# Attention block: the newest chunk's first piece waits for less, upsampling additions at other steps, rectifier inside VectorE's last additions

## The chip, the cores and the metric

The kernel runs on one core of one Trainium2 chip. Its five engines work from queues of their own and wait for one another by semaphores: TensorE (PE in the rows; PEld is its weight load), VectorE (DVE), ScalarE (ACT), GpSimd (POOL) and SyncE (SP), which here only starts transfers. The metric is the time of one execution on the device in microseconds. Tiles live in SBUF; matmuls write into eight PSUM banks.

## The reference

Input `x` is 4 images of 256 channels of 128 x 128, in float32. Each goes through this:

```python
shortcut = x
out = bilinear_resize(x, H // 2, W // 2)
out = relu(bn(conv1x1(out, conv1_w), bn1_s, bn1_b))
out = att(out, q_w, q_b, k_w, k_b, v_w, v_b, att_gamma)   # softmax(q^T k) over 64*64 positions
out = relu(bn(out, bn2_s, bn2_b))
out = bn(conv1x1(out, conv2_w), bn3_s, bn3_b)
out = bilinear_resize(out, H, W)
return relu(out + shortcut)
```

Attention runs over 4096 positions with 32 channels for queries and keys and 256 for values. All of it is computed to float32 accuracy; the kernel splits weights of the softmax and values into high and low halves of 16 bits.

## The kernel before

**Batches and blocks.** Every image is a batch `b` with two parts. `enter(b)` computes the first convolution, queries, keys and values of the batch. Then eight blocks `n` (also called chunks; `c` is 0, 1 or 7 and says which program text is used, and `g = b * 8 + n`) take 512 query positions each. A block has 32 steps `t`, one for each 128 keys. What each engine does in a step is written out by hand in its `blk`.

**TensorE in a step.** For four row tiles `it` it multiplies `ph` (high halves of the weights) by `vh` and `vl`, and `pl` (low halves) by `vh`, into `acc[it]` (lines 1062 to 1064). After row tile 2 it makes the energies of step t + 3 in `et`, two banks in turn (L940), which wait until `pl` of the step two before is made. Most steps also have one or two pair units (L928), which find the maxima for the next block in banks `emx` and `wrk`. Steps 30 and 31 are merged. The transposes of the block before come at steps 1 and 5 (L952), its second convolution at 20 and 22 (L960).

**ScalarE.** For each step it takes two exponentials of `et` (L443, L444), and for each pair of units the positive part `above` (L452). In between stand the batch norm and rectifier `relu_h` (L456), `bn3`, which writes the convolution's result into `win` and counts `y_rdy` up twice a chunk (L475), the copies of `osb` (L574), the final rectifier of upsampled pieces (L481) and the stores (L486).

**VectorE.** In its iteration t it makes `pl` of step t + 2 (`low_parts`, L710), at every second unit `pair_max` (L689, a custom operation), at steps 2 and 6 the `residual` (L720), at 31 the reciprocals of row sums (`row_sum`, L809) and its copy of `osb` (L830), and last in an iteration, what `T_ADD` puts there.

**Pieces.** Each block also upsamples four pieces j of chunks finished earlier, of 8 output rows each. GpSimd computes `up_chain` (L335 to L352): row differences `rd` and `rt`, then `y2`, `cd` and `ct`. There is one `y2` and one `ct`, so `y2` of the next piece waits for the first two additions of the piece before, and `ct` for the last two. Then VectorE adds `y2` to the two halves of the shortcut rows in `xres` (parts 0 and 1, L737) and `ct` to the same halves (parts 2 and 3, L740). Part 0 waits for the whole `up_chain`. `T_ADD[j][part]` gives the step. ScalarE rectifies at `T_RELU[j]` and stores one step later; piece 3 is rectified at step 1 of the next block. Pieces 0 to 2 are of the chunk three back, piece 3 of the chunk two back. There are no pieces 0 to 2 before block 3 and no piece 3 before block 2 of batch 0.

**Downsampling.** Between the pieces, in the first three batches, GpSimd downsamples four pieces of the next batch (`down_piece`, L315 to L325), so its order is up 0, down 0, up 1, down 1, up 2, down 2, up 3, down 3. SP loads their inputs into `xin` and the shortcuts into four slots of `xres`; a slot's load waits for the store of what was in it.

**The end.** In the last block two more pieces are added by `T_ADD_LAST`. Nine late pieces follow after TensorE's last work, shared by GpSimd and VectorE; VectorE makes all their additions, ScalarE rectifies and stores.

Of the kernel before, what the change touches and what calls it, by code (L numbers as in the profile page):

```python
# [18 lines left out]
NB = N // IB  # L19
# [14 lines left out]
SHIFT = 256.0  # L34
V_TOP = 2.0 ** 14
BN = 1.0 / (1.0 + 1e-5) ** 0.5

DN, DV, UP = 6, 5, 5
V_OF = (3, 2, 3, 2, 2, 2, 2, 2)
# [2 lines left out]
def attention_block_kernel(nc, x, w1, s1, b1, wq, bq, wk, bk, wv, bv, gamma, s2, b2, w2, s3, b3,  # L42
                           ident_d, down_w, up_w, out):
    with ExitStack() as ctx:
# [73 lines left out]
        stored = [sem(f"stored{i}") for i in range(4)]  # L118
        down_p, down_v, rows_w = sem("down_p"), sem("down_v"), sem("rows_w")
        up_p, up_v = sem("up_p"), sem("up_v")  # L120
        up_added, up_relu = sem("up_added"), sem("up_relu")
        c1_rdy, c1_done = sem("c1_rdy"), sem("c1_done")
        qk_rdy, qk_hi, qk_done = sem("qk_rdy"), sem("qk_hi"), sem("qk_done")
        v_rdy, vh_rdy, v_done, vscale = sem("v_rdy"), sem("vh_rdy"), sem("v_done"), sem("vscale")
# [231 lines left out]
        def _(pool):  # L356
# [47 lines left out]
            def blk(b, n, c):  # L404
                ups = {j: (u, un, pr, k) for j, u, _, un, pr, k in up_pieces(b, n, c)}
                g = b * NB + n
                for j in range(max(PIECES, len(ups))):
                    if j in ups:
                        if j == 3:
                            pool.wait_ge(y_rdy, g * 2)  # L410
                        u = ups[j][0]
                        up_piece(*ups[j], u * UP, u)
                    if not (isinstance(b, int) and b == B - 1):

                        i = n * PIECES + j
                        fills = P_ALL // 2
                        pool.wait_ge(xin_ld[j % 2], b * (16 * NB * PIECES // 2) + n * 32 + (16 * (fills + j // 2 + 1)))
                        small = (n * 2 + j // 2) * (DR // 2)
                        dst = xr[:, bass.ds(n, 1), j % 2, (j // 2) * (DR // 2):(j // 2 + 1) * (DR // 2), :]
                        down_piece(pool, ops, down_p, down_count(b + 1, i), xin[:, j % 2], dd[:],  # L420
                                   dst.rearrange("p o r c -> p (o r) c"), small)
# [14 lines left out]
        def _(act):  # L436
# [38 lines left out]
                    done = ops.activation(dst, src, ACT.Identity, bias=par[:, B3, half:half + 1], scale=par[:, S3, half:half + 1])  # L475
                done.then_inc(y_rdy, 1)

            def final_relu(j, i):

                act.wait_ge(up_added, i * 2 + 2)  # L480
                ops.activation(xres[:, xslot(j)], xres[:, xslot(j)], ACT.Relu).then_inc(up_relu, 1)  # L481

            def store(j, i, b, n, k):
                half, row = piece_rows(n, k)
                act.wait_ge(up_relu, i + 1)
                act.dma_start(dram_rows(out, b, half, row, UR), xres[:, xslot(j)]).then_inc(stored[xslot(j)], 16)  # L486

            def weight_rows(ck, js):
# [58 lines left out]
            def blk(b, n, c):  # L547
                g = held(act, b * NB + n)
                s0 = held(act, g * JT)
                ups = {j: (u, ub, un, k) for j, u, ub, un, _, k in up_pieces(b, n, c)}  # L550
                before = {}
                if not (isinstance(g, int) and g < 3):
                    before = {j: (u, ub, un, k) for j, u, ub, un, _, k in
                              (up_pieces(b, n - 1, c - 1) if c else up_pieces(b - 1, NB - 1, NB - 1))}
                t_cv, t_relu = (T_CV_LAST, T_RELU_LAST) if is_last(b, c) else (T_CV, T_RELU if c < NB - 1 else T_RELU_7)
                for t in range(JT):
                    if c > 0 and t in (T_OT[0] + 2, T_OT[1] + 2):
                        relu_h(g - 1, T_OT.index(t - 2))
                    if t in (t_cv[0] + 1, t_cv[1] + 1) and not (isinstance(g, int) and g == 0):
                        bn3(g - 1, (c - 1) % 2, t_cv.index(t - 1), c == 1, c == 0)  # L560
                    if t in t_relu and t_relu.index(t) in ups:
                        final_relu(t_relu.index(t), ups[t_relu.index(t)][0])
                    if t - 1 in t_relu and t_relu.index(t - 1) in ups:
                        store(t_relu.index(t - 1), *ups[t_relu.index(t - 1)])

                    if t == T_RELU_BEFORE and 3 in before:
                        final_relu(3, before[3][0])
                    if t == T_RELU_BEFORE + 1 and 3 in before:
                        store(3, *before[3])
                    if t == JT - 1:  # L570

                        for it in range(IT - 1):
                            act.wait_ge(rl_rdy, g * IT + (it + 1))
                            ops.activation(osb[:, it, :], acc[it][:, 0:C], ACT.Copy, scale=rl[:, it:it + 1]).then_inc(acc_out, 1)  # L574
                    if c < NB - 1:
                        for u in EMAX_AT[t]:
                            if u % 2 == 0:
                                difference_above(b, n + 1, u)
                    if t + AHEAD < JT or c < NB - 1:
                        weights_of(s0 + (t + AHEAD), (t + AHEAD) % JT)  # L580
# [5 lines left out]
            for half in range(2):  # L586
                relu_h(NB * B - 1, half)
            ups = list(up_pieces(B - 1, NB - 1, NB - 1))
            for j, u, ub, un, _, k in ups[len(T_RELU_LAST):]:
                final_relu(j, u)  # L590
                store(j, u, ub, un, k)
            for half in range(2):
                bn3(NB * B - 1, (NB - 1) % 2, half, False, True)
            for i, u in enumerate(LATE_ORDER):
                j, ub, un, _, k = late_piece(u)
                final_relu(j, LATE + i)
                store(j, LATE + i, ub, un, k)

        @block.vector
        def _(dve):  # L600
# [127 lines left out]
            def add_part(j, u, part, i, y2, ct):  # L728
# [6 lines left out]
                if part < 2:  # L735
                    xs4 = xs.rearrange("p r (c two) -> p r c two", two=2)
                    ops.tensor_tensor(xs4, xs4, y2[:, rs].unsqueeze(3).broadcast_to([P, UR // 2, S, 2]), ALU.add).then_inc(up_v, 1)  # L737
                else:
                    dve.wait_ge(up_v, i * 2 + (part - 1))
                    ops.tensor_tensor(xs, xs, ct[:, rs].rearrange("p r c two -> p r (c two)"), ALU.add).then_inc(up_added, 1)  # L740

            def qk_low(b, ck):

# [67 lines left out]
            def blk(b, n, c):  # L811
# [6 lines left out]
                for t in range(JT):  # L818
# [5 lines left out]
                    if units and len(EMAX_AT[t]) == 1:  # L824
                        pair_max(b, n + 1, units[0])
                    if t == JT - 1:
                        for it in range(IT):
                            row_sum(g, it)
                        dve.wait_ge(rl_rdy, g * IT + IT)
                        ops.tensor_scalar(osb[:, IT - 1, :], acc[IT - 1][:, 0:C], rl[:, IT - 1:IT], None,  # L830
                                          ALU.mult).then_inc(acc_out_v, 1)
                    if t + 2 < JT or more:
                        low_parts(s0 + (t + 2), (t + 2) % JT)
                    if units and len(EMAX_AT[t]) == 2:
                        pair_max(b, n + 1, units[0])
                    if c > 0 and t in (T_OT[0] + 1, T_OT[1] + 1):
# [337 lines left out]
FIRST_AFTER_CONV2 = min(_u for _u in _wrk_units if _u > EMAX_AT[T_CV[1]][0])  # L1174
T_SHIFT = 26
T_MT = 27
T_ADD = ((4, 5, 6, 8), (12, 13, 14, 16), (18, 20, 21, 22), (28, 28, 29, 29))
T_RELU = (9, 17, 24)
T_ADD_7 = ((4, 5, 6, 8), (14, 15, 16, 17), (22, 23, 24, 25), (29, 30, 31, 31))
T_RELU_7 = (9, 19, 27)  # L1180
T_RELU_BEFORE = 1

MORE_LAST = 2
T_CV_LAST = (12, 14)
T_ADD_LAST = ((1, 3, 4, 5), (7, 8, 9, 10), (11, 12, 13, 14), (20, 21, 22, 23), (25, 26, 27, 28), (30, 30, 31, 31))
T_RELU_LAST = (6, 11, 16, 24, 29)
LATE = PIECES * (NB * B - 1) - 11 + PIECES + MORE_LAST
LATE_ORDER = tuple(LATE + i for i in (0, 2, 1, 4, 3, 6, 5, 8, 7))
LATE_POOL = tuple(LATE + i for i in (0, 1, 3, 5, 7))
# [35 lines left out]
```

## Time and profile before

| | |
|---|---|
| median of 3 runs | 2481.05 us (2480.34 to 2482.93) |
| the profiled execution | 2478.03 us |
| its span, first to last instruction | 2476.2 us |
| mean granted TensorE clock | 0.982 |
| TensorE matmuls busy | 2290.5 us, 92% |
| VectorE busy | 1807.0 us, 73% |
| ScalarE busy | 1800.5 us, 73% |
| GpSimd busy | 1694.7 us, 68% |

The busy shares are means over stages; a row of a window or a timeline tells of one stage. A matmul is shown longer than the distance to the next, because the engine works on several at once. A releaser is named behind an arrow: `PE et L940 <- DVE pl L710` is TensorE at line 940, which waited for VectorE's instruction of line 710.

### The profile page before, as it was taken

How to read it: one execution, taken by the hardware profiler on the slowest of the kernel's cores; microseconds unless marked ns; L12 is line 12 of the kernel's file. 1: busy time of each engine (PE TensorE's matmuls, PEld its weight loads, DVE VectorE, ACT ScalarE, POOL GpSimd, SP SyncE). 2: the span in 40 equal slices, each digit the busy share in tenths (PEclk: the TensorE clock that was granted, in tenths of full speed). 3: DMA queues.
4: the chain of work that ended last, by engine and by line, in shares of the span. 5: the costliest groups of instructions: out<-in, count | busy, mean ns of one | idle time of the engine just before them, and what ended most of it. 6: DMA issues, size and time to landing. Idle time of an engine off the chain costs nothing.

```text
span 2476.2 us, 48184 instructions
## 1 busy us (share of the span) xinstructions
PE 2290.5 (92%) x15914; PEld 1636.0 (66%) x15914; DVE 1807.0 (73%) x3339; ACT 1800.5 (73%) x3345; POOL 1694.7 (68%) x1617
## 2 busy tenths in 40 slices
PE   4799999999999999999999999999999999999981
PEld 2377777777567777777747777777756777777760
DVE  7855577777777777777686777777777777777779
ACT  5467778877557787777747877887755778778762
POOL 7991088888548888888845888888853444444475
PEclk9899999999999999999999999999999999999995
DMA  6321022222102222222302222222310222111133
GB/s 206 100 77 35 1 76 102 102 94 102 51 26 95 94 102 102 102 93 98 108 1 78 95 93 102 102 102 93 106 39 18 69 69 68 68 60 63 64 103 136
DMA packets 59129, 204.11 MB, mean 82 GB/s; under 512 B 8736, under 2 KB 9824, under 8 KB 58976
## 3 DMA queue, kind: packets, MB, share of 16 engines
q1 hardware_dynamic: 40544, 135.26, 16.9%
q10 hardware_dynamic: 18432, 67.12, 6.6%
q8 instruction: 58, 0.95, 0.2%
q14 instruction: 95, 0.78, 0.1%
HBM read 135.24 MB, written 67.11 MB: 82 GB/s over the span
## 4 chain that ended last, share of the span: by engine, by line
PE 73%; DVE 15%; issue 5%; ACT 4%; POOL 3%; SPq 1%; DMA 0%; DVEq 0%; ACTq 0%; POOLq 0%
PE acc L1062 15%; PE acc L1064 14%; PE acc L1063 14%; PE et L940 8%; PE emx L928 5%; PE wrk L960 4%; PE acc L988 4%; DVE xres L740 4%; DVE xres L737 3%; DVE pl L710 3%; PE wrk L928 2%; PE acc L980 2%; ACT above L452 2%; PE wrk L952 1%; DVE am L757 1%
## 5 line engine op out<-in xcount | busy, mean ns | idle before, releaser
L1062 PE MATMUL acc<-vh,ph 128*128 128x257 f16 x4096 | 1120.5, 274 | 21.5 <-DVE pl L710 20.1
L1064 PE MATMUL acc<-vh,pl 128*128 128x257 f16 x4096 | 1116.2, 273 | 0.0
L1063 PE MATMUL acc<-vl,ph 128*128 128x256 f16 x4096 | 1111.0, 271 | 0.0
L710 DVE TENSOR_TENSOR pl<-et,ph 128x512 f16<-128x512 f32 x1024 | 701.6, 686 | 140.3 <-ACT et L444 135.7
L443 ACT ACTIVATE ph<-et 128x512 f16<-128x512 f32 x1024 | 610.5, 596 | 259.0 <-PE et L940 255.9
L444 ACT ACTIVATE et<-et 128x512 f32<-128x512 f32 x1024 | 608.9, 595 | 0.0
L1063 PEld LDWEIGHTS acc<-vl,ph 128*128 128x128 f16 x4096 | 401.1, 98 | 274.9 <-issue 20.5
L1062 PEld LDWEIGHTS acc<-vh,ph 128*128 128x128 f16 x4096 | 400.3, 98 | 95.5 <-DVE pl L710 26.7
L1064 PEld LDWEIGHTS acc<-vh,pl 128*128 128x128 f16 x4096 | 395.6, 97 | 56.1
L940 PE MATMUL et<-qs,ks 98*128 (+1 forms) x1024 | 390.3, 381 | 30.4 <-DVE pl L710 30.3
L352 POOL TENSOR_TENSOR ct<-cd,uw 128x512 f32<-128x512 f32 x248 | 317.7, 1302 | 79.3 <-DVE xres L740 73.0
L335 POOL TENSOR_TENSOR rd<-win 128x320 f32<-128x320 f32 x124 | 119.3, 962 | 318.0 <-ACT win L475 317.8
L689 DVE CUSTOM_DVE_ANT_0 above<-wrk,above 128x512 f32<-128x512 f32 x308 | 212.4, 690 | 146.4 <-PE wrk L928 95.2
L452 ACT ACTIVATE above<-emx 128x512 f32<-128x512 f32 x448 | 265.5, 593 | 39.0 <-PE emx L928 30.5
L345 POOL TENSOR_TENSOR y<-win,rt 128x512 f32<-128x512 f32 x124 | 170.1, 1372 | 174.6 <-DVE xres L737 167.2
L689 DVE CUSTOM_DVE_ANT_0 above<-emx,above 128x512 f32<-128x512 f32 x140 | 96.8, 692 | 220.5 <-PE emx L928 220.5
L737 DVE TENSOR_TENSOR xres<-xres,y 128x512 f32<-128x512 f32 x248 | 225.7, 921 | 4.3 <-POOL ct L352 4.3
L740 DVE TENSOR_TENSOR xres<-xres,ct 128x512 f32<-128x512 f32 x248 | 204.7, 836 | 0.0
L928 PE MATMUL emx<-kd,qm 96*128 96x512 f16 x448 | 171.0, 382 | 5.1 <-ACT above L452 4.9
L481 ACT ACTIVATE xres<-xres 128x1024 f32<-128x1024 f32 x128 | 134.1, 1048 | 50.6 <-DVE xres L740 50.5
L340 POOL TENSOR_TENSOR rt<-rd,uw 128x256 f32<-128x256 f32 x248 | 162.9, 678 | 9.7
L319 POOL TENSOR_TENSOR xin<-xin 128x512 f32<-128x512 f32 x110 | 146.7, 1334 | 8.6
(130 smaller groups left out, 2847.5 us busy)
## 6 DMA issues: line engine op xcount, KB each, us to landing
xres<-in_x SPq DMA_DIRECT2D x146, 512.0 KB, 4.5
out<-xres ACTq DMA_DIRECT2D x128, 512.0 KB, 2.6
xin<-in_x SPq DMA_DIRECT2D x110, 512.0 KB, 3.7
osb<-in_L_conv_conv_w SPq DMA_DIRECT2D x1, 256.0 KB, 7.6
osb<-in_L_conv_v_w SPq DMA_DIRECT2D x1, 256.0 KB, 7.6
hbuf<-in_L_conv_conv_w SPq DMA_DIRECT2D x1, 256.0 KB, 7.5
ident<-identity SPq DMA_DIRECT2D x1, 64.0 KB, 7.7
uw<-up_weights SPq DMA_DIRECT2D x1, 64.0 KB, 2.5
```

The lines of the kernel that those rows point to most:

```text
L352: last = ops.tensor_tensor(ct_[:, :, :, parity], cd_[:, :, parity:parity + S], wt, ALU.mult)
L443: ops.activation(ph[:, t % 4, :], et[t % 2][:, :], ACT.Exp)
L444: ops.activation(et[t % 2][:, :], et[t % 2][:, :], ACT.Exp).then_inc(p_rdy, 1)
L452: ops.activation(above[:, p % 2, :], (emx, wrk)[MAX_BANK[u]][:, :], ACT.Relu).then_inc(above_rdy, 1)
L689: ops.tensor_tensor_reduce(above[:, p % 2, :], (emx, wrk)[MAX_BANK[u]][:, :], above[:, p % 2, :], 1.0, LOWEST, ALU.add, ALU.max, mx[:, p % ...
L710: ops.tensor_tensor(pl[:, t % 4, :], et[t % 2][:, :], ph[:, t % 4, :], ALU.subtract).then_inc(pl_rdy, 1)
L740: ops.tensor_tensor(xs, xs, ct[:, rs].rearrange("p r c two -> p r (c two)"), ALU.add).then_inc(up_added, 1)
L928: mm(bank[:, :], qm[:, it * P:(it + 1) * P], keys, start=True, stop=True).then_inc(emx_rdy if taken else above_in, 1)
L940: mm(et[t % 2][:, :], ks[0:3 * D + 2, t * P:(t + 1) * P], qs[0:3 * D + 2, bass.ds(n * IB, IB)], start=True, stop=True).then_inc(et_rdy, 1)
L1062: mm(acc[it][:, 0:C + 1], ph[:, tt % 4, pt], vh[:, tt, 0:C + 1], start=tt == 0, stop=False)
L1063: mm(acc[it][:, 0:C], ph[:, tt % 4, pt], vl[:, tt, :], start=False, stop=False)
L1064: last = mm(acc[it][:, 0:C + 1], pl[:, tt % 4, pt], vh[:, tt, 0:C + 1], start=False, stop=tt == JT - 1)
```

## The change

The wait of `y_rdy` that GpSimd makes before piece 3 asks for one chunk less (`g * 2 - 2`, and also stands before piece 1); the wait for the newest chunk, `g * 2`, moves to piece 5 of the last block. Additions of the blocks 0 to 6 stand at other steps, at most one in each. `T_ADD_7` and `T_ADD_LAST` stay as they are. `final_relu` goes: parts 2 and 3 are a custom operation on VectorE that adds and limits the sum to between 0 and the largest float32. The store waits for the additions and stands one step earlier, where the rectifier stood. In VectorE's last iteration `low_parts` moves ahead of the last `row_sum` and its copy of `osb`.

```diff
@@ -34,6 +34,7 @@
 SHIFT = 256.0
 V_TOP = 2.0 ** 14
 BN = 1.0 / (1.0 + 1e-5) ** 0.5
+HUGE = 3.4028234663852886e38
 
 DN, DV, UP = 6, 5, 5
 V_OF = (3, 2, 3, 2, 2, 2, 2, 2)
@@ -118,7 +119,7 @@
         stored = [sem(f"stored{i}") for i in range(4)]
         down_p, down_v, rows_w = sem("down_p"), sem("down_v"), sem("rows_w")
         up_p, up_v = sem("up_p"), sem("up_v")
-        up_added, up_relu = sem("up_added"), sem("up_relu")
+        up_added = sem("up_added")
         c1_rdy, c1_done = sem("c1_rdy"), sem("c1_done")
         qk_rdy, qk_hi, qk_done = sem("qk_rdy"), sem("qk_hi"), sem("qk_done")
         v_rdy, vh_rdy, v_done, vscale = sem("v_rdy"), sem("vh_rdy"), sem("v_done"), sem("vscale")
@@ -406,7 +407,9 @@
                 g = b * NB + n
                 for j in range(max(PIECES, len(ups))):
                     if j in ups:
-                        if j == 3:
+                        if j in (1, 3):
+                            pool.wait_ge(y_rdy, g * 2 - 2)
+                        if j == 5:
                             pool.wait_ge(y_rdy, g * 2)
                         u = ups[j][0]
                         up_piece(*ups[j], u * UP, u)
@@ -475,14 +478,9 @@
                     done = ops.activation(dst, src, ACT.Identity, bias=par[:, B3, half:half + 1], scale=par[:, S3, half:half + 1])
                 done.then_inc(y_rdy, 1)
 
-            def final_relu(j, i):
-
-                act.wait_ge(up_added, i * 2 + 2)
-                ops.activation(xres[:, xslot(j)], xres[:, xslot(j)], ACT.Relu).then_inc(up_relu, 1)
-
             def store(j, i, b, n, k):
                 half, row = piece_rows(n, k)
-                act.wait_ge(up_relu, i + 1)
+                act.wait_ge(up_added, i * 2 + 2)
                 act.dma_start(dram_rows(out, b, half, row, UR), xres[:, xslot(j)]).then_inc(stored[xslot(j)], 16)
 
             def weight_rows(ck, js):
@@ -552,20 +550,16 @@
                 if not (isinstance(g, int) and g < 3):
                     before = {j: (u, ub, un, k) for j, u, ub, un, _, k in
                               (up_pieces(b, n - 1, c - 1) if c else up_pieces(b - 1, NB - 1, NB - 1))}
-                t_cv, t_relu = (T_CV_LAST, T_RELU_LAST) if is_last(b, c) else (T_CV, T_RELU if c < NB - 1 else T_RELU_7)
+                t_cv, t_store = (T_CV_LAST, T_STORE_LAST) if is_last(b, c) else (T_CV, T_STORE if c < NB - 1 else T_STORE_7)
                 for t in range(JT):
                     if c > 0 and t in (T_OT[0] + 2, T_OT[1] + 2):
                         relu_h(g - 1, T_OT.index(t - 2))
                     if t in (t_cv[0] + 1, t_cv[1] + 1) and not (isinstance(g, int) and g == 0):
                         bn3(g - 1, (c - 1) % 2, t_cv.index(t - 1), c == 1, c == 0)
-                    if t in t_relu and t_relu.index(t) in ups:
-                        final_relu(t_relu.index(t), ups[t_relu.index(t)][0])
-                    if t - 1 in t_relu and t_relu.index(t - 1) in ups:
-                        store(t_relu.index(t - 1), *ups[t_relu.index(t - 1)])
-
-                    if t == T_RELU_BEFORE and 3 in before:
-                        final_relu(3, before[3][0])
-                    if t == T_RELU_BEFORE + 1 and 3 in before:
+                    if t in t_store and t_store.index(t) in ups:
+                        store(t_store.index(t), *ups[t_store.index(t)])
+
+                    if t == T_STORE_BEFORE and 3 in before:
                         store(3, *before[3])
                     if t == JT - 1:
 
@@ -586,14 +580,12 @@
             for half in range(2):
                 relu_h(NB * B - 1, half)
             ups = list(up_pieces(B - 1, NB - 1, NB - 1))
-            for j, u, ub, un, _, k in ups[len(T_RELU_LAST):]:
-                final_relu(j, u)
+            for j, u, ub, un, _, k in ups[len(T_STORE_LAST):]:
                 store(j, u, ub, un, k)
             for half in range(2):
                 bn3(NB * B - 1, (NB - 1) % 2, half, False, True)
             for i, u in enumerate(LATE_ORDER):
                 j, ub, un, _, k = late_piece(u)
-                final_relu(j, LATE + i)
                 store(j, LATE + i, ub, un, k)
 
         @block.vector
@@ -737,7 +729,8 @@
                     ops.tensor_tensor(xs4, xs4, y2[:, rs].unsqueeze(3).broadcast_to([P, UR // 2, S, 2]), ALU.add).then_inc(up_v, 1)
                 else:
                     dve.wait_ge(up_v, i * 2 + (part - 1))
-                    ops.tensor_tensor(xs, xs, ct[:, rs].rearrange("p r c two -> p r (c two)"), ALU.add).then_inc(up_added, 1)
+                    ops._custom_dve(bass.dve_ops.TENSOR_ADD_SAT, out=xs, in0=xs, in1=ct[:, rs].rearrange("p r c two -> p r (c two)"),
+                                    s0=HUGE, s1=0.0).then_inc(up_added, 1)
 
             def qk_low(b, ck):
 
@@ -824,13 +817,15 @@
                     if units and len(EMAX_AT[t]) == 1:
                         pair_max(b, n + 1, units[0])
                     if t == JT - 1:
-                        for it in range(IT):
+                        for it in range(IT - 1):
                             row_sum(g, it)
+                    if t + 2 < JT or more:
+                        low_parts(s0 + (t + 2), (t + 2) % JT)
+                    if t == JT - 1:
+                        row_sum(g, IT - 1)
                         dve.wait_ge(rl_rdy, g * IT + IT)
                         ops.tensor_scalar(osb[:, IT - 1, :], acc[IT - 1][:, 0:C], rl[:, IT - 1:IT], None,
                                           ALU.mult).then_inc(acc_out_v, 1)
-                    if t + 2 < JT or more:
-                        low_parts(s0 + (t + 2), (t + 2) % JT)
                     if units and len(EMAX_AT[t]) == 2:
                         pair_max(b, n + 1, units[0])
                     if c > 0 and t in (T_OT[0] + 1, T_OT[1] + 1):
@@ -1174,16 +1169,16 @@
 FIRST_AFTER_CONV2 = min(_u for _u in _wrk_units if _u > EMAX_AT[T_CV[1]][0])
 T_SHIFT = 26
 T_MT = 27
-T_ADD = ((4, 5, 6, 8), (12, 13, 14, 16), (18, 20, 21, 22), (28, 28, 29, 29))
-T_RELU = (9, 17, 24)
+T_ADD = ((1, 3, 4, 5), (7, 8, 10, 11), (13, 14, 16, 17), (21, 22, 23, 27))
+T_STORE = (9, 17, 24)
 T_ADD_7 = ((4, 5, 6, 8), (14, 15, 16, 17), (22, 23, 24, 25), (29, 30, 31, 31))
-T_RELU_7 = (9, 19, 27)
-T_RELU_BEFORE = 1
+T_STORE_7 = (9, 19, 27)
+T_STORE_BEFORE = 1
 
 MORE_LAST = 2
 T_CV_LAST = (12, 14)
 T_ADD_LAST = ((1, 3, 4, 5), (7, 8, 9, 10), (11, 12, 13, 14), (20, 21, 22, 23), (25, 26, 27, 28), (30, 30, 31, 31))
-T_RELU_LAST = (6, 11, 16, 24, 29)
+T_STORE_LAST = (6, 11, 16, 24, 29)
 LATE = PIECES * (NB * B - 1) - 11 + PIECES + MORE_LAST
 LATE_ORDER = tuple(LATE + i for i in (0, 2, 1, 4, 3, 6, 5, 8, 7))
 LATE_POOL = tuple(LATE + i for i in (0, 1, 3, 5, 7))
```

## Rows read from the trace of the kernel before

**Rows 1.** The page: busy time of the engines, and one group of instructions
```profile
PE 2290.5 (92%) x15914; PEld 1636.0 (66%) x15914; DVE 1807.0 (73%) x3339; ACT 1800.5 (73%) x3345; POOL 1694.7 (68%) x1617
...
L689 DVE CUSTOM_DVE_ANT_0 above<-emx,above 128x512 f32<-128x512 f32 x140 | 96.8, 692 | 220.5 <-PE emx L928 220.5
```

**Rows 2.** Windows of one block each: start:end, length, busy us of each engine
```profile
789.13:853.17 64.04, 62.01 (x470) 45.43 (x469) 48.19 (x93) 51.00 (x94) 55.10 (x53) 1.00 0.29 100
1965.24:2029.28 64.04, 61.85 (x470) 45.60 (x469) 46.50 (x94) 51.02 (x94) 28.30 (x29) 1.00 0.20 67
```

**Rows 3.** Waits inside 789.13 to 853.17: us in total, times, longest
```profile
POOL rd L335 <- ACT win L475: 5.2, 1, 5.2
...
PE acc L1062 <- DVE pl L710: 0.9, 1, 0.9
```

**Rows 4.** Timeline of VectorE, block's end: start us, us, instructions merged
```profile
846.44 2.35 DVE L737 TENSOR_TENSOR xres<-xres,y 128x512 f32<-128x512 f32 x2
...
849.32 1.81 DVE L740 TENSOR_TENSOR xres<-xres,ct 128x512 f32<-128x512 f32 x2
```

**Rows 5.** Timeline of TensorE: start us, us, instruction, idle time before it
```profile
786.06 0.27 PE L1062 MATMUL acc<-vh,ph 128*128 128x257 f16 x1
786.17 0.27 PE L1063 MATMUL acc<-vl,ph 128*128 128x256 f16 x1
...
798.09 0.38 PE L940 MATMUL et<-qs,ks 98*128 x1
...
809.13 0.39 PE L928 MATMUL emx<-kd,qm 96*128 96x512 f16 x1 [0.22 <-ACT above L452]
...
818.71 0.38 PE L940 MATMUL et<-qs,ks 98*128 x1
...
851.88 0.39 PE L940 MATMUL et<-qs,ks 98*128 x1 [0.39 <-DVE pl L710]
...
854.40 0.39 PE L940 MATMUL et<-qs,ks 98*128 x1 [0.49 <-DVE pl L710]
```

**Rows 6.** Timeline of ScalarE at step 9
```profile
807.53 1.06 ACT L481 ACTIVATE xres<-xres 128x1024 f32<-128x1024 f32 x1 [0.35 <-DVE xres L740]
```

**Rows 7.** Timeline of GpSimd: first instructions of some stages
```profile
807.64 2.55 POOL L352 TENSOR_TENSOR ct<-cd,uw 128x512 f32<-128x512 f32 x2 [0.94 <-DVE xres L740]
810.15 1.27 POOL L315 TENSOR_TENSOR xin<-xin 128x512 f32<-128x512 f32 x1
...
816.50 1.36 POOL L335 TENSOR_TENSOR rd<-win 128x320 f32<-128x320 f32 x1
...
825.06 1.27 POOL L315 TENSOR_TENSOR xin<-xin 128x512 f32<-128x512 f32 x1
...
837.01 0.86 POOL L335 TENSOR_TENSOR rd<-win 128x320 f32<-128x320 f32 x1 [5.25 <-ACT win L475]
...
844.18 1.27 POOL L315 TENSOR_TENSOR xin<-xin 128x512 f32<-128x512 f32 x1
```

**Rows 8.** Timeline of VectorE: additions and a low_parts
```profile
800.41 0.68 DVE L737 TENSOR_TENSOR xres<-xres,y 128x512 f32<-128x512 f32 x1
...
806.82 0.68 DVE L740 TENSOR_TENSOR xres<-xres,ct 128x512 f32<-128x512 f32 x1
...
816.46 0.68 DVE L737 TENSOR_TENSOR xres<-xres,y 128x512 f32<-128x512 f32 x1
...
817.67 0.68 DVE L710 TENSOR_TENSOR pl<-et,ph 128x512 f16<-128x512 f32 x1
...
832.72 0.68 DVE L740 TENSOR_TENSOR xres<-xres,ct 128x512 f32<-128x512 f32 x1
```

**Rows 9.** Waits inside 1965.24 to 2029.28, a block of batch 3
```profile
PE et L940 <- DVE pl L710: 1.9, 2, 1.4
```

**Rows 10.** Timelines of VectorE and ScalarE at the program's end
```profile
2470.70 1.28 DVE L740 TENSOR_TENSOR xres<-xres,ct 128x512 f32<-128x512 f32 x2
...
2472.01 1.06 ACT L481 ACTIVATE xres<-xres 128x1024 f32<-128x1024 f32 x1 [1.35 <-DVE xres L740]
```

## The prediction

> **What bounds the kernel.** I read the page first. TensorE is busy 92% of the span, no other engine over 73% [rows 1]. Only two things can therefore move the time: gaps on TensorE inside the attention blocks, and the tail after its last matmul. Next I read windows of one block each. A block of the middle batches lasts 64.04 us, and GpSimd is busy for 55.10 of them. In the last batch it is as long, but GpSimd works 28.30 us, since there is nothing left to downsample [rows 2]. Then came the waits inside one middle block [rows 3]: TensorE waits 0.9 us for VectorE's `pl` ahead of an `acc` matmul, and GpSimd waits 5.2 us for `bn3` of the newest chunk.
>
> The timelines say where. A matmul of 257 columns is shown 0.27 us long while the next one follows after 0.11 (786.06 and 786.17, rows 5), so 0.16 us of each TensorE gap is hidden; I add 0.16 to each idle time shown. I count four gaps in a block that have to do with the change.
> - End of the block: piece 3's two pairs of additions stand at 846.44 (2.35 us) and 849.32 (1.81 us), with `low_parts` waiting between and behind them [rows 4]. TensorE stops for 0.9 + 0.16 = 1.0 us for step 31 [rows 3].
> - `low_parts` for step 0 of the next block is late too, then the one for step 1, which comes behind `row_sum(3)` and the copy of `osb`. Two waits ahead of `energies`, at 851.88 and 854.40, show 0.39 and 0.49 us [rows 5]; with the hidden part 0.88 + 0.32 = 1.2 us.
> - Step 9: ScalarE's rectifier, 1.06 us at 807.53 [rows 6], stands ahead of `above` in its queue, and the pair unit at 809.13 has waited 0.22 + 0.16 = 0.4 us [rows 5].
> - The rectifier at step 24 should do the same in small; no gap is listed, I take 0.1.
>
> **Which blocks.** The code gives 32 blocks. Blocks 0 to 6 of a batch use `T_ADD`; block 7 uses `T_ADD_7` or `T_ADD_LAST`, which stay. All four pieces beside downsampling: blocks 3 to 6 of batch 0 and 0 to 6 of batches 1 and 2, that is 18. All four without downsampling: 7, in batch 3. Blocks 0 and 1 of batch 0 have no piece, block 2 only piece 3.
>
> **Gains of a block.** With no additions at 28 and 29, `low_parts` of step 31 and of step 0 wait only for ScalarE's exponentials, so the 1.0 goes. With `low_parts` of step 1 ahead of `row_sum(3)`, it runs while TensorE finishes row tile 3, so most of the 1.2 goes; the query copy, still behind `osb`, keeps the third one tight, so I take 1.1, with bounds 0.55 (only the first half) and 1.2. The rectifiers give 0.5. Sum 2.6 us. In the last batch the two waits at the block's end are 1.9 us [rows 9], with the hidden part 2.2; less 0.1, plus 0.5, again 2.6.
>
> **Cost of the moved additions themselves.** Each is 0.68 us when alone. Most of the new steps have VectorE idle behind `low_parts`, waiting for TensorE or ScalarE; that idle time hides them. At 7, 10 and 27 it is short and a clash with GpSimd may show: 0.1 us a block, bounds 0 and 0.5. The rectifying add is not in the trace in this form. The nearest rows are the plain add and the other custom operation (0.692 us for 512 columns, one input from PSUM, rows 1). I take 0.68; bounds nothing more and twice as long.
>
> **The new wait.** This is the term that decides. GpSimd's order in a block is up 0, down 0, up 1, down 1, up 2, down 2, up 3, down 3, with one `y2` and one `ct`. Its last step of up 1 writes `ct`, so it waits for the fourth addition of piece 0, now at step 5. VectorE wants the whole of up 2 at step 13, before piece 2's first addition. Between lie `ct` of up 1, down 1 and all of up 2. Before, it was from step 8 to step 18 and nobody waited. The narrower `y_rdy` wait cannot help here, since `ct` is held by the addition, not by `bn3`.
>
> In times of the block from 789.13: the step-5 slot is at 800.41 [rows 8]. GpSimd follows an addition's start by 807.64 - 806.82 = 0.82 us. From there `ct`, down 1 and up 2 took 825.06 - 807.64 = 17.42 us [rows 7], with four additions across it (12, 13, 14, 16); the new stretch has four too (7, 8, 10, 11). So up 2 is ready at 800.41 + 0.82 + 17.42 = 818.65. VectorE makes that addition at 816.46 today; it will stand for over 2 us. Behind it in VectorE's queue are the `pair_max` of step 14 and `low_parts` of step 16, which ended 817.67 + 0.68 - 816.46 = 1.89 us after the addition began. TensorE can issue the energies of step 18 about 0.1 us later: 818.65 + 1.89 + 0.1 = 820.64. Now they start at 818.71 [rows 5], and without the 0.4 at step 9 they would at 818.31. A stall of 2.3 us. It counts from the energies at 798.09, to which both ends are tied, so what changes at the block's start does not enter.
>
> Bounds: up 3 alone ran 844.18 - 837.01 = 7.17 us, but up 2 with three additions beside it 825.06 - 816.50 = 8.56 [rows 7], so a clash costs GpSimd about 0.45. With none of the four clashes the stall is 2.3 - 1.8 = 0.5; if each cost a whole 0.68 it is 2.3 + 0.9 = 3.2. The Trainium skill (SBUF — State Buffer, "SBUF: two separate sides") says that VectorE with two SBUF inputs and GpSimd share a port pair as an exclusive lock, held for a whole instruction. By that rule, read to the letter, the stall would be 3.2; the 0.45 agrees with it in kind, not in full size.
>
> Piece 3 just fits: down 2 as down 1 (816.50 - 810.15 = 6.35 us) and up 3 as up 2 (8.56) make it ready at 818.65 + 14.9 = 833.6, and the addition of step 21, now at 832.72 [rows 8], comes 2.3 - 0.5 later, at 834.5. In batch 3 there is no down 1 and the wait doesn't arise.
>
> **Other queues.** SP's shortcut loads wait for the stores of the piece before in the same slot; these come one step earlier than now. Input loads follow GpSimd's downsampling two pieces ahead. ScalarE's stores stand at least three steps behind the additions they wait for, so none stops the exponentials behind it. All nothing.
>
> **Tail.** VectorE's chain of late pieces is unchanged. At the very end the last addition ends, the rectifier at 2472.01 takes 1.06 us and only then comes the store [rows 10]: -1.0 us.
>
> **Sum.** 18 blocks at -2.6 + 2.3 + 0.1 = -0.2: -3.6. 7 blocks at -2.6 + 0.1 = -2.5: -17.5. Blocks 0 and 1 of batch 0 have only the half behind `row_sum(3)`, -0.55 each, and block 2 -1.0 - 1.1: together -3.2. Tail -1.0. In all -25.3. The profiled execution took 2478.03 (span 2476.2 and 1.8 around it), the median is 2481.05, 3 above; the difference carries over. 2481.05 - 25.3 = 2455.8, said as 2456.
>
> **Rivals.**
> - A, the wait at step 13 barely shows, because GpSimd and VectorE seldom clash when spread out: 1.8 us less in 18 blocks, -32, so about 2424 to 2438. For it: additions in rows 8 are at 0.68 each. Against: GpSimd has hardly a pause from 5 to 13. Chance 0.14.
> - B, the lock bites in full (3.2 us, +16) or only half of the 1.1 at the block's end returns (+0.55 in 26 blocks, +14): 2470 to 2478, some of it no change. For it: clashes do stretch GpSimd's work in rows 7, and the row sums lie tight. Chance 0.16. (This is where the page of the Trainium skill on SBUF, named above, would put the stall.) Both together would give 2486, which I leave out of the range.
> - C, the other side: the rectifying add is twice as long (1.2 us). Then the step-5 addition frees `ct` 0.5 later and each of four clashes takes 0.5 more, so the stall grows by 2.6 and 18 blocks by 47 us: about 2500. Break-even is a stall 1.4 us longer, that is an add about 0.3 us longer. Against: the other custom operation keeps the plain pace. Chance 0.07.
> - D, the moved waits do nothing, as the gaps return elsewhere with VectorE as the bound: 2478 to 2483. In rows 2 it has room, GpSimd too. Chance 0.03.
>
> The forecast has 0.60, with 2442 to 2468 as its own range. 0.2% is 5 us, about what a measurement here can tell from no change. Faster 0.85, same 0.07, slower 0.08. The range goes from inside A to inside B, 2432 to 2475.
>
> **What would show it.** Right: no rectifier rows; TensorE's waits at steps 9 and 31 gone; a VectorE wait of 2 to 4 us for `ct` before piece 2's first addition in 18 blocks and in none of batch 3; middle blocks near 63.9 us and last-batch ones near 61.5. Wrong, if middle blocks fall to 62 (A), if L740 is longer than 0.9 us in the mean (C), or if gaps at the block's end stay (B).

## The result, and the profile after

The changed kernel takes 2514.17 us (2509.12 to 2516.76, 4 runs) against 2480.7 for the one before: a ratio of 1.0133, 95% interval 1.0121 to 1.0145. It is 33 us slower, where 25 us faster was forecast. One of the ten runs of a later kernel, the one with the narrower wait alone, took 3446 us at a granted clock of 0.65; its ratio leaves that run out.

The page of the changed kernel, first its busy times, the granted clock in 40 slices, the chain's shares and the two groups of additions:

```profile
PE 2319.5 (92%) x15914; PEld 1657.8 (66%) x15914; DVE 1857.2 (74%) x3339; ACT 1698.6 (68%) x3217; POOL 1673.5 (67%) x1617
...
PEclk8899999999999999999999999999999999999995
...
PE 68%; POOL 15%; DVE 10%; issue 4%; ACT 2%; SPq 1%; DMA 0%; DVEq 0%; POOLq 0%; ACTq 0%
...
L729 DVE TENSOR_TENSOR xres<-xres,y 128x512 f32<-128x512 f32 x248 | 268.2, 1084 | 75.9 <-POOL ct L353 75.8
...
L732 DVE CUSTOM_DVE_ANT_0 xres<-xres,ct 128x512 f32<-128x512 f32 x248 | 232.8, 941 | 0.0
```

TensorE is as busy in share as in [rows 1]. But GpSimd has 15% of the chain, and L729 has waited 75.8 us for `ct`. The row of the clock shows tenths, rounded down, and has nines all through the attention blocks, as it had in the kernel before. It is too coarse for what follows; the mean granted clock is 0.962 where it was 0.982. Windows of two middle blocks and one block of batch 3 (length, then busy us of PE, PEld, DVE, ACT and POOL, the granted clock, DMA):

```profile
805.04:873.08 68.04, 64.55 (x470) 46.90 (x469) 50.46 (x94) 48.02 (x90) 54.31 (x53) 0.95 0.28 94
873.08:939.55 66.47, 62.98 (x470) 46.20 (x469) 52.03 (x93) 48.24 (x92) 54.24 (x53) 0.97 0.28 95
1984.90:2046.10 61.20, 61.11 (x469) 45.85 (x468) 47.01 (x94) 48.56 (x94) 28.05 (x29) 1.00 0.21 70
```

Against [rows 2] the middle blocks are 4.0 and 2.4 us longer, the one of batch 3 is 2.8 us shorter. All 18 middle blocks (those with all four pieces beside downsampling) are near one of these two. The 16 that lie between two copies of `osb` take 67.2 us in the mean, and the same blocks of the kernel before mostly 64.2. So the gains are real, and the middle blocks pay more than they get. The waits inside the block from 873.08:

```profile
DVE xres L729 <- POOL ct L353: 3.7, 1, 3.7
PE et L935 <- DVE pl L702: 3.4, 1, 3.4
```

TensorE's waits of [rows 3, 5] at the block's end and at step 9 are gone. In their place one wait of VectorE and one of TensorE stand, at the steps forecast. GpSimd's, VectorE's and TensorE's timelines through it, in that order:

```profile
885.05 2.55 POOL L353 TENSOR_TENSOR ct<-cd,uw 128x512 f32<-128x512 f32 x2 [1.89 <-DVE xres L732]
...
899.80 2.54 POOL L353 TENSOR_TENSOR ct<-cd,uw 128x512 f32<-128x512 f32 x2
902.30 1.26 POOL L316 TENSOR_TENSOR xin<-xin 128x512 f32<-128x512 f32 x1
```

```profile
882.48 1.23 DVE L732 CUSTOM_DVE_ANT_0 xres<-xres,ct 128x512 f32<-128x512 f32 x1
...
884.23 0.68 DVE L732 CUSTOM_DVE_ANT_0 xres<-xres,ct 128x512 f32<-128x512 f32 x1
...
898.02 0.68 DVE L702 TENSOR_TENSOR pl<-et,ph 128x512 f16<-128x512 f32 x1
902.37 1.73 DVE L729 TENSOR_TENSOR xres<-xres,y 128x512 f32<-128x512 f32 x1 [3.67 <-POOL ct L353]
904.03 0.68 DVE L681 CUSTOM_DVE_ANT_0 above<-wrk,above 128x512 f32<-128x512 f32 x1
...
904.64 0.68 DVE L702 TENSOR_TENSOR pl<-et,ph 128x512 f16<-128x512 f32 x1
```

```profile
881.39 0.38 PE L935 MATMUL et<-qs,ks 98*128 x1
...
901.82 0.27 PE L1059 MATMUL acc<-vh,pl 128*128 128x257 f16 x1
905.46 0.61 PE L935 MATMUL et<-qs,ks 98*128 x1 [3.37 <-DVE pl L702]
```

Read it from the fourth addition of piece 0 at 884.23: GpSimd's `ct` starts 0.82 us later, and up 2 is complete when down 2 starts at 902.30, 17.25 us on. VectorE's addition has waited since `low_parts` at 898.02. It then takes 1.73 us instead of 0.68, because GpSimd started down 2 at 902.30, 0.07 us ahead of it. Behind it come `pair_max` (904.03) and `low_parts` of step 16 (904.64 to 905.32), and TensorE's energies at 905.46 have waited 3.37 us (3.53 with the hidden part). These energies themselves take 0.61 us where others take 0.38. The windows around them say why:

```profile
898.00:901.40 3.40, 3.40 (x29) 2.55 (x27) 0.70 (x3) 2.44 (x5) 3.24 (x4) 1.00 0.16 65
905.40:907.00 1.60, 1.54 (x6) 0.81 (x7) 1.60 (x2) 0.89 (x2) 1.52 (x2) 0.50 0.00 0
910.60:916.00 5.40, 5.40 (x44) 4.00 (x42) 5.35 (x11) 4.37 (x8) 5.17 (x6) 1.00 0.77 283
```

The granted clock is 1.00 before the stop, 0.50 behind it (1.2 in place of 2.4 GHz), and 1.00 again some microseconds later. The trace has such a stop of 3.4 us, and a clock that falls to half within 1.3 us of the stop's end, before or behind it, in all 18 middle blocks.

### The profile page after: what moved, and what is told of

Same layout as the page of the kernel before. It is cut to its first block, busy times and chain, and to the rows that moved or that the text cites. A ratio compares the mean times of both kernels' runs of the same rounds, so it can differ in the third digit from the quotient of the medians.

```text
span 2512.5 us, 48056 instructions
## 1 busy us (share of the span) xinstructions
PE 2319.5 (92%) x15914; PEld 1657.8 (66%) x15914; DVE 1857.2 (74%) x3339; ACT 1698.6 (68%) x3217; POOL 1673.5 (67%) x1617
## 4 chain that ended last, share of the span: by engine, by line
PE 68%; POOL 15%; DVE 10%; issue 4%; ACT 2%; SPq 1%; DMA 0%; DVEq 0%; POOLq 0%; ACTq 0%
PE acc L1057 14%; PE acc L1059 14%; PE acc L1058 14%; PE et L935 7%; PE wrk L955 4%; POOL ct L353 4%; PE emx L923 4%; PE acc L983 4%; PE wrk L923 2%; DVE xres L732 2%; PE acc L975 2%; POOL xin L320 2%; POOL xin L318 1%; POOL xin L316 1%; POOL rt L341 1%
## 5 line engine op out<-in xcount | busy, mean ns | idle before, releaser
L1057 PE MATMUL acc<-vh,ph 128*128 128x257 f16 x4096 | 1133.5, 277 | 2.4 <-DVE vl L756 1.4
L1059 PE MATMUL acc<-vh,pl 128*128 128x257 f16 x4096 | 1129.1, 276 | 0.0
L1058 PE MATMUL acc<-vl,ph 128*128 128x256 f16 x4096 | 1124.1, 274 | 0.0
L935 PE MATMUL et<-qs,ks 98*128 (+1 forms) x1024 | 396.4, 387 | 62.5 <-DVE pl L702 61.7
L346 POOL TENSOR_TENSOR y<-win,rt 128x512 f32<-128x512 f32 x124 | 161.6, 1303 | 289.6 <-DVE xres L729 284.4
L729 DVE TENSOR_TENSOR xres<-xres,y 128x512 f32<-128x512 f32 x248 | 268.2, 1084 | 75.9 <-POOL ct L353 75.8
L732 DVE CUSTOM_DVE_ANT_0 xres<-xres,ct 128x512 f32<-128x512 f32 x248 | 232.8, 941 | 0.0
L341 POOL TENSOR_TENSOR rt<-rd,uw 128x256 f32<-128x256 f32 x248 | 172.6, 717 | 9.7
L336 POOL TENSOR_TENSOR rd<-win 128x320 f32<-128x320 f32 x124 | 129.3, 1043 | 58.8 <-ACT win L478 58.5
L935 PEld LDWEIGHTS et<-qs,ks 98*128 98x128 f16 x1024 | 100.0, 98 | 91.0 <-issue 67.2
L348 POOL TENSOR_TENSOR cd<-y 128x504 f32<-128x504 f32 x124 | 144.0, 1162 | 9.7
```

Source lines behind the costliest of these rows:

```text
L732: ops._custom_dve(bass.dve_ops.TENSOR_ADD_SAT, out=xs, in0=xs, in1=ct[:, rs].rearrange("p r c two -> p r (c two)"), s0=HUGE, s1=0.0).then_ ...
L935: mm(et[t % 2][:, :], ks[0:3 * D + 2, t * P:(t + 1) * P], qs[0:3 * D + 2, bass.ds(n * IB, IB)], start=True, stop=True).then_inc(et_rdy, 1)
L1057: mm(acc[it][:, 0:C + 1], ph[:, tt % 4, pt], vh[:, tt, 0:C + 1], start=tt == 0, stop=False)
L1058: mm(acc[it][:, 0:C], ph[:, tt % 4, pt], vl[:, tt, :], start=False, stop=False)
L1059: last = mm(acc[it][:, 0:C + 1], pl[:, tt % 4, pt], vh[:, tt, 0:C + 1], start=False, stop=tt == JT - 1)
```

## The experiments

Each ratio is to the kernel before, measured on the same chip. It took 2480.2 to 2481.2 us on all of them, so the times can be set side by side too. The cause to be tested: `ct` is held until step 5, so up 2 comes too late for step 13; that stops TensorE, and the stop halves the clock.

**Piece 2 two steps later.** One line of the changed kernel:

```diff
-T_ADD = ((1, 3, 4, 5), (7, 8, 10, 11), (13, 14, 16, 17), (21, 22, 23, 27))
+T_ADD = ((1, 3, 4, 5), (7, 8, 10, 11), (15, 16, 17, 18), (21, 22, 23, 27))
```

> The changed kernel with piece 2's additions at steps 15, 16, 17, 18 in place of 13, 14, 16, 17, nothing else. Theory (ct is held until the step-5 addition, so up 2 is ready 0.82 + 17.25 us after it, too late for step 13; the halved clock comes from the 3.5 us stop of TensorE): ready before the slot of step 15, so no stop, no half clock, middle blocks near 61.6 us and about 2409 us in all, faster than both kernels. Rival 1 (VectorE's longer clashes with GpSimd and the rectifying addition are the cause): these stay, so it stays above 2490. Rival 2 (the wait only moves with the piece): a wait of 2 us or more at step 15 and about 2500.

Measured 2415.1 us, ratio 0.9737 (0.972 to 0.9753): 99 us less than the changed kernel, from the place of a few additions. A middle block's window, one of its waits, and the group of rectifying additions:

```profile
775.80:837.48 61.68, 61.56 (x470) 45.62 (x469) 49.65 (x93) 47.96 (x90) 55.22 (x53) 1.00 0.30 103
```

```profile
DVE xres L729 <- POOL ct L353: 1.2, 1, 1.2
```

```profile
L732 DVE CUSTOM_DVE_ANT_0 xres<-xres,ct 128x512 f32<-128x512 f32 x248 | 212.1, 858 | 0.0
```

VectorE still waits 1.2 us for `ct`, which I had not expected, but TensorE doesn't stop: `low_parts` has room for it at this step. Rival 2 is out. The addition behind the wait still takes 1.74 us and the rectifying addition is still there, which speaks against rival 1; but its mean fell from 941 to 858 ns, so fewer of the clashes are left. The two buffers below settle this rival.

**One step later.** The same with `(14, 15, 16, 17)`.

> The changed kernel with piece 2's additions at 14, 15, 16, 17. Theory: up 2 is still about 2.5 us late for the slot, but low_parts of step 17 is due one step later than that of step 16, so TensorE stops for about 0.9 us in 18 blocks, not 3.5, and the clock stays at its full level: about 2425 us. Rival 1 (clashes, not the wait): above 2490 as before. Rival 3 (any stop there halves the clock): half clock in each middle block and about 2460.

Measured 2448.34 us, ratio 0.987 (0.9854 to 0.9887). Too low a price for the stop was forecast again:

```profile
785.10:848.71 63.61, 61.85 (x470) 45.47 (x469) 50.57 (x94) 47.99 (x90) 54.45 (x53) 1.00 0.29 100
```

```profile
PE et L935 <- DVE pl L702: 1.6, 2, 0.9
...
DVE xres L729 <- POOL ct L353: 1.0, 1, 1.0
```

VectorE waits only 1.0 us, and TensorE stops twice for 1.6 us in all (1.9 with the hidden parts), not once for 0.9. The second addition clashes like the first. The clock stays at 1.00. Rival 3 gives the nearer total, 2460, but by a half clock that isn't there.

**Two buffers.** The steps as changed, but two `y2` and two `ct`:

```diff
-        y2 = sb("y2", [P, UR, S])
...
-        ct = sb("ct", [P, UR, S, 2])
+        y2s = [sb(f"y2_{i}", [P, UR, S]) for i in range(2)]
+        cts = [sb(f"ct_{i}", [P, UR, S, 2]) for i in range(2)]
...
-                        up_piece(*ups[j], u * UP, u)
+                        up_piece(*ups[j], u * UP, u - 1, j % 2)
```

> The changed kernel, steps as they are, with two y2 and two ct in turn, so GpSimd's next piece waits for the additions of the piece two before. Theory: up 2 no longer hangs on step 5, the wait at step 13 is gone, about 2405 to 2415 us. Rival (GpSimd as a whole is too slow for these steps, whatever its buffers): the wait shrinks by less than half and the time stays above 2480.

Measured 2404.88 us, ratio 0.9693 (0.9676 to 0.9709). The window of a middle block, and the group of rectifying additions:

```profile
773.52:835.25 61.73, 61.52 (x470) 45.62 (x469) 50.93 (x94) 47.95 (x90) 57.52 (x55) 1.00 0.29 103
...
L734 DVE CUSTOM_DVE_ANT_0 xres<-xres,ct 128x512 f32<-128x512 f32 x248 | 231.4, 936 | 0.0
```

Piece 2 is added at 13 here and nothing stops. The rectifying additions take 936 ns in the mean, as long as the 941 of the changed kernel, so their clashes are not what made it slow. GpSimd is fast enough; it was only held by one buffer. With the first experiment this settles the place of the wait. Middle blocks are no shorter than there. Of the 10 us between the two, 4.3 come from the program's last block (52.96 us between its copies of `osb`, 57.28 with one buffer); the rest I have not traced to a place.

**Two buffers and piece 2 at 15.** Both edits together.

> Both mends together: two y2 and two ct in turn, and piece 2's additions at 15, 16, 17, 18. Theory: with either one the wait is gone, so together they bring nothing more than the last block's 4 us that the buffers alone gave: 2400 to 2406. Rival (GpSimd still held something back with two buffers at step 13): under 2398.

Measured 2405.9 us (2404.91 to 2407.24), ratio 0.9699 (0.9683 to 0.9715), the same as the buffers alone: the two mend the same wait.

**The stop filled with work.** The changed kernel with matmuls ahead of the energies that wait:

```diff
+                            if t == 15 and more and not (isinstance(b, int) and b == B - 1):
+                                for _ in range(26):
+                                    mm(acc[0][:, C + 2:2 * C], ident_h[:, :], vl[:, 0, 0:C - 2], start=False, stop=False)
                             energies(s0 + e, e % JT, n + e // JT)
```

> The changed kernel with 26 matmuls of 254 columns ahead of the energies of step 18, in blocks 0 to 6 of the first three batches, into columns that nothing reads; they fill about 2.8 of the 3.5 us in which TensorE stands. Theory (the stop and the half clock behind it are two prices): the wait for VectorE's pl shrinks to about 0.7 us while the block's length is set as before by GpSimd and VectorE; the half clock goes, about 2 us in each of 18 blocks, and three blocks without a stop pay 2.8 us: about 2514 - 37 + 8 = 2485. Rival (the half clock has another cause than the stop): half clock in the same blocks, about 2522.

Measured 2486.15 us, ratio 1.0023 (1.0012 to 1.0034), 28 us less than the changed kernel for 2.98 us more of work in each of 21 blocks. TensorE's timeline at the stop, and the block's window:

```profile
895.99 2.98 PE L1070 MATMUL acc<-vl,ident_h 128*128 128x254 f16 x26
899.53 0.39 PE L935 MATMUL et<-qs,ks 98*128 x1 [0.56 <-DVE pl L702]
```

```profile
867.13:932.46 65.33, 64.62 (x496) 48.09 (x495) 51.32 (x93) 48.30 (x92) 54.65 (x53) 1.00 0.28 97
```

VectorE's wait is as long as ever, the block is 1.1 us shorter than the shorter kind in the changed kernel, and the clock is 1.00, in all 21 blocks that have the filling. So the half clock is a price by itself, and it hangs on TensorE having nothing to do. Blocks without a stop (three, in batch 0) pay for the filling: about 8 us. Without them the clock accounts for 28 + 8 = 36 us, 2.0 for each of 18 blocks.

**The clash taken away.** GpSimd stays off its next instruction until the addition has been made. The two lines stand ahead of each down 2 of the first three batches:

```diff
+                        if j == 2 and j in ups:
+                            pool.wait_ge(up_v, ups[j][0] * 2 + 1)
```

> The changed kernel with GpSimd held ahead of down 2 until VectorE's first addition of piece 2 is done, so this addition no longer meets a GpSimd instruction. Theory (1.05 us of the stop are this clash): the addition takes 0.68 and not 1.73 us, TensorE's stop falls from 3.53 to about 2.5 us; about 2495 us if the half clock stays, about 2458 if it goes too. Rival (the clash doesn't matter, GpSimd's later pieces do): the stop stays or moves to piece 3, no gain.

Measured 2490.55 us, ratio 1.0038 (1.0024 to 1.0052). VectorE's timeline in a middle block, TensorE's wait there, and the windows of this block and the next:

```profile
892.89 0.69 DVE L731 TENSOR_TENSOR xres<-xres,y 128x512 f32<-128x512 f32 x1 [3.65 <-POOL ct L353]
893.50 0.69 DVE L683 CUSTOM_DVE_ANT_0 above<-wrk,above 128x512 f32<-128x512 f32 x1
...
894.11 0.69 DVE L704 TENSOR_TENSOR pl<-et,ph 128x512 f16<-128x512 f32 x1
```

```profile
PE et L937 <- DVE pl L704: 2.3, 1, 2.3
```

```profile
863.61:929.33 65.72, 63.28 (x470) 46.35 (x469) 49.53 (x93) 48.30 (x92) 54.26 (x53) 0.97 0.28 96
929.33:993.42 64.09, 61.65 (x470) 45.63 (x469) 49.21 (x94) 48.28 (x92) 54.05 (x53) 1.00 0.28 98
```

The addition takes 0.69 us, and TensorE's stop is 2.3 us shown, 2.5 in all, as expected. The clock is another matter. All 18 middle blocks have this stop, but the lower clock follows it only in every other block of a batch, ten in all. Such a block takes 65.7 us, the others 64.1. So half the clock costs 1.7 us here, and a stop of this length brings it only sometimes. What decides in which block stays open.

The gain of 24 us is near the 19 expected, but partly by luck. A middle block is 2.3 us shorter in the mean (64.9 against 67.2), about 41 us in 18: 1.05 a block from the clash, the rest from the clock. Block 7 of each batch pays some of it back. There the new wait holds GpSimd for an addition at step 22, and the block takes 56.2 us in place of 53.0:

```profile
625.52 1.27 POOL L316 TENSOR_TENSOR xin<-xin 128x512 f32<-128x512 f32 x1 [5.78 <-DVE xres L731]
```

That is 10 us in three blocks; the remaining 7 stand between the batches, where TensorE has new stops of 3.8 to 3.9 us.

**The parts one by one.** Four kernels, each with a part of the change.

The changed kernel with `T_ADD` as before:

> The changed kernel with T_ADD as it was before; the narrower wait, the rectifying addition and the order of low_parts and row_sum stay. Theory: all the loss goes; left are the rectifiers' 0.5 us, the 0.65 us behind row_sum(3), and 1.5 us at the program's end: 25 blocks at about -1.1 and so about 2450 us. Rival 1 (the rectifying addition is the cause): still slower than the kernel before.

Measured 2448.74 us, ratio 0.9865 (0.9848 to 0.9881), as forecast. All of the loss is in the new steps, and rival 1 is out.

The kernel before with the rectifying addition and the earlier stores alone:

> The kernel before with the rectifying addition and the earlier stores alone. Theory: the 0.4 and 0.1 us at steps 9 and 24 go in 25 blocks and 1 us at the end: about -13 us, 2468. Rival 1 (the custom addition is longer or clashes worse): slower than before.

Measured 2468.79 us, ratio 0.9955 (0.9938 to 0.9972). Its group of rectifying additions, next to the group of the plain ones in the kernel before:

```profile
L730 DVE CUSTOM_DVE_ANT_0 xres<-xres,ct 128x512 f32<-128x512 f32 x248 | 204.5, 836 | 0.0
```

```profile
L740 DVE TENSOR_TENSOR xres<-xres,ct 128x512 f32<-128x512 f32 x248 | 204.7, 836 | 0.0
```

Both have a mean of 836 ns over 248: at the same steps the rectifier inside the addition costs nothing. The 941 ns of the changed kernel are clashes.

The kernel before with the narrower wait alone:

> The kernel before with the narrower y_rdy wait alone. Theory: GpSimd runs some 5 us ahead at piece 3 and nobody waits for it there, so no difference beyond 2 us. Rival: other clashes with VectorE's additions move the time by 5 us or more.

Measured 2478.86 us, ratio 0.9995 (0.9985 to 1.0005): nothing.

The kernel before with `low_parts` ahead of the last `row_sum` alone:

> The kernel before with one part of the change: low_parts ahead of the last row_sum and its copy of osb. Theory: of the two waits at the block's end the second (0.65 us) goes, in 28 boundaries inside batches: about -17 us, 2464. Rival (the additions at step 29 make the same low_parts late anyway): under -5 us.

Measured 2470.35 us, ratio 0.9962 (0.9948 to 0.9976): 10 us, between the two. And piece 2 at 15 with the old order:

```diff
-                        for it in range(IT - 1):
+                        for it in range(IT):
                             row_sum(g, it)
+                        dve.wait_ge(rl_rdy, g * IT + IT)
+                        ops.tensor_scalar(osb[:, IT - 1, :], acc[IT - 1][:, 0:C], rl[:, IT - 1:IT], None,
+                                          ALU.mult).then_inc(acc_out_v, 1)
                     if t + 2 < JT or more:
                         low_parts(s0 + (t + 2), (t + 2) % JT)
```

> The changed kernel with piece 2 at 15, 16, 17, 18 and the order of low_parts and the last row_sum as it was before. Theory: 0.65 us slower in each of 28 boundaries than with the new order, about 2427 us if that one takes 2409. Rival (with no additions at 28 and 29 the order no longer matters): the same time as with the new order.

Measured 2433.78 us, ratio 0.9819 (0.9803 to 0.9835): 18.7 us slower than with the new order, 0.67 in each of 28 boundaries. Its runs spread from 2429.5 to 2437.3 us, so the middle blocks of the two traces are the surer measure: 62.3 against 61.7. The 0.65 us of the forecast stand.

## Why the prediction was wrong

The mechanism, its place and the blocks it hits were right; two prices were not. By the prediction's own terms:

- **Gains, 2.6 us less 0.1 a block:** right. With the wait out of the way (piece 2 at 15) a middle block takes 61.68 us against 64.2, 2.5 less; in batch 3, where the wait cannot arise, 61.20 against 64.04, 2.8 less. The parts alone gave their shares: rectifier 11.4 us where 13 were expected, order of the row sums 18.7 us once nothing else delays that `low_parts`.
- **GpSimd's stretch, 17.42 us:** right, 17.25 measured. The four clashes cost GpSimd 0.3 to 0.5 us each (line 318 takes 1.37 us beside an addition and 1.04 without one), near the 0.45 assumed. The 3.2 us of my bound, which I took for the rule of the Trainium skill read to the letter, charged GpSimd a whole addition per clash; that is over a microsecond too much for this stretch.
- **From VectorE's addition to the energies, 1.89 us: this step failed.** I took it from an addition of 0.68 us that met nobody. The one behind the wait is released in the moment in which GpSimd goes on to its next instruction, so it clashes in all 18 middle blocks: 1.73 us. It started 0.07 us behind an instruction of 1.26 us and ended 0.54 us after that one's end, so here VectorE, the second to start, did the waiting. I had priced only what clashes cost GpSimd. From 902.37 to 905.32 are 2.95 us, 1.06 more than 1.89; taking only the clash away gave back 1.05 of the stop. The other 0.15 of 3.53 - 2.3 is a sum of small terms. The addition of step 5 starts 2.84 us behind the energies at 881.39, where I had 2.32, because the addition of step 4 clashes (1.23 us at 882.48): 0.5 more. GpSimd's stretch is 0.2 shorter, and TensorE would have come to the waiting energies 0.3 us later than I had it.
- **A stop costs its length: this step failed as well, and no rival had it.** I had put the clock at nothing. Behind each of the 18 stops TensorE ran at half its clock for a while, which is worth 2.0 us a block by the filled stop; and 67.2 us of a mean middle block less 61.68 and 3.53 leave 2.0 too. The Trainium skill has the rule that I left out (TensorE: Matmul & The Clock Gate, "HAM oscillation — how this bites in real kernels"): a gap in TensorE's work can throw it back to the lower clock, and then every round pays for it. The trace agrees, with 0.50 granted at 905.4 behind a stop of 3.53 us. The forecast stop of 2.3 us was near the 2.5 us of the run without the clash, and that one halved the clock in ten blocks, at 1.7 us each. So even at my own price the clock was worth about 17 us, which makes 2473, just inside my range.
- **Sum:** 18 blocks at 1.2 for the longer stop and 2.0 for the clock are 58 us. 2456 + 58 = 2514, as measured. The longer stop alone would have given about 2477, the clock behind a stop of the forecast length about 2473; both lie near the range's upper end of 2475. The longer stop also brings the lower clock in all blocks and not in every other one.
- **Rivals.** B had the size of the stop (3.2) by another road, the lock charging every clash in full; the stretch of 17.25 us rules that road out. C is out by the equal means of 836 ns. The sign that I had given for it, a mean above 0.9 us, did appear (941 ns), but by clashes and not by a longer operation: it could not tell the two apart. A is out by the wait itself. None ended near 2514, since all priced the stop alone.
- **Other queues and the tail:** nothing came from SP or ScalarE. From the last copy of `osb` to the end the kernel before takes 2476.2 - 2406.8 = 69.4 us, the changed one 2512.5 - 2444.5 = 68.0; -1.4 where -1.0 was forecast. The last `osb` copies are the last starts in these rows:

```profile
L830 DVE TENSOR_SCALAR osb<-acc,rl x32: 482/484/485, 203.8 to 2406.8; 128x256 f32<-128x256 f32 x32
```

```profile
L827 DVE TENSOR_SCALAR osb<-acc,rl x32: 483/484/485, 204.6 to 2444.5; 128x256 f32<-128x256 f32 x32
```

## What to carry to other kernels

When work is moved in a schedule written by hand, follow each single buffer round its loop: the release at one step, the producer's whole queue up to the next use, and the slot of that use. Here 0.8 + 17.3 us stood in a place of 14.5 (from the addition at 884.23 to 898.70, when VectorE was free), and two steps more, or a second buffer, turned 1.3% slower into 2.6 or 3.1% faster. Price what starts right behind a wait by its clashed duration, because both engines are let go at once. A sign of being wrong should tell a longer operation from a clashed one. And ask of each stop of TensorE whether the clock falls with it.

## What the runs showed of the hardware

- A stop of TensorE of 3.4 us shown in each middle block brought half the clock in 18 of 18 blocks, one of 2.3 us shown (2.5 in all) in 10 of 18, and two of 0.8 and 0.9 us (1.6 together) in none. With matmuls in the stop whose results nobody reads the clock stayed at 1.00.
- The length of one stop doesn't settle it. Between two batches of the changed kernel TensorE stops for 1.58 us shown ahead of line 1011; behind it the clock was 0.50 in one batch and 1.00 in the next:

```profile
704.00:706.00 2.00, 2.00 (x5) 0.67 (x4) 1.00 (x2) 0.00 (x0) 0.00 (x0) 0.50 0.00 0
1316.00:1318.00 2.00, 2.00 (x7) 0.70 (x5) 0.98 (x2) 0.00 (x0) 0.00 (x0) 1.00 0.04 8
```

- An addition of VectorE with two inputs from SBUF takes 0.68 us alone and 1.73 us when GpSimd has started an instruction of 1.26 us 0.07 us before it.
- The custom operation that adds and limits takes as long as the plain addition, 836 ns in the mean of 248 at the same steps.
